# Causal masking by GpSimd and a fused VectorE maximum in place of TensorE's mask products

## The reference

```
x   = table[ids]                                  # (16, 512, 128)
x   = softmax(x W1 (W2 x^T) / sqrt(512)) x        # low-rank mixing, rank 10
two routed experts per sequence (one spatial, one temporal, of 4 each), by the mean token
S   = MHA(LN(x)),        8 heads of 16, no mask   # spatial expert's weights
T   = xt + MHA(LN'(x)),  8 heads of 16, causal    # temporal expert's weights
C   = MHA(q from S, k and v from T), no mask      # shared weights
x   = x + C ;  out = x + MLP(LN(x)), 128 -> 512 -> 128
```

## Time and profile before

| | |
|---|---|
| median of 3 runs | 1761.52 us (1761.07 to 1762.53) |
| profiled execution | 1758.67 us, its span 1756.8 us |
| TensorE busy | 1585.8 us, 90% of the span, 9686 matmuls |
| VectorE busy | 1239.0 us, 71%, 2943 instructions |
| ScalarE busy | 1118.9 us, 64%, 2185 |
| GpSimd busy | 948.1 us, 54%, 1249 |
| mean granted TensorE clock | 0.942 of full speed |

### The profile page before, as it was taken

One profiled execution on the slowest core, in us unless ns is written; L12 is line 12 of the kernel. 1 busy time (PEld: TensorE's weight loads), 2 busy tenths in 40 slices (PEclk: granted clock), 3 DMA queues, 4 the chain that ended last, 5 costly groups with the idle time before them and its releaser, 6 DMA issues. The chain is left out here.

```text
span 1756.8 us, 38227 instructions
## 1 busy us (share of the span) xinstructions
PE 1585.8 (90%) x9686; PEld 728.2 (41%) x9686; DVE 1239.0 (71%) x2943; ACT 1118.9 (64%) x2185; POOL 948.1 (54%) x1249
## 2 busy tenths in 40 slices
PE   3758957999999999999999999999999999975998
PEld 1117942334434444444434444434434444221675
DVE  6886858478687777878687777878687787452442
ACT  3324751747777778777777778687777778724333
POOL 7832443556656656656656656656656655332443
PEclk9768966989999999999999999999999999967999
DMA  2221126356446546546546546546545535030221
GB/s 51 72 48 32 48 57 76 55 71 86 64 67 77 74 54 79 71 55 83 68 63 75 75 55 76 73 56 80 69 65 72 77 50 68 2 37 26 61 65 54
DMA packets 134642, 109.26 MB, mean 62 GB/s; under 512 B 24128, under 2 KB 127552, under 8 KB 134592
## 3 DMA queue, kind: packets, MB, share of 16 engines
q1 hardware_dynamic: 132544, 104.45, 41.0%
q0 software_dynamic: 2048, 4.20, 0.9%
HBM read 19.26 MB, written 8.39 MB: 16 GB/s over the span
## 5 line engine op out<-in xcount | busy, mean ns | idle before, releaser
L1064 ACT ACTIVATE probs<-psum 128x512 f32<-128x512 f32 (+3 forms) x1536 | 744.0, 552 | 315.1 <-PE psum L1178 203.0
L961 DVE TENSOR_REDUCE mx_S<-psum 128x1 f32<-128x512 f32 x512 | 325.0, 682 | 71.4 <-PE psum L1154 69.8
L961 DVE TENSOR_REDUCE mx_C<-psum 128x1 f32<-128x512 f32 x512 | 321.5, 677 | 63.5 <-PE psum L1154 63.5
L961 DVE TENSOR_REDUCE mx_T<-psum 128x1 f32<-128x128 f32 (+3 forms) x512 | 243.1, 488 | 133.2 <-PE psum L1157 122.6
L864 POOL CAST parts_q<-f_q 128x512 bf16<-128x512 f32 x48 | 29.3, 611 | 340.1 <-ACT f_q L1055 340.1
L1154 PE MATMUL psum<-ks_C,qs_C 96*128 96x512 bf16 x512 | 202.2, 398 | 4.9 <-DVE mx_C L961 2.6
L1154 PE MATMUL psum<-ks_S,qs_S 96*128 96x512 bf16 x512 | 199.1, 394 | 5.1 <-DVE mx_S L961 4.1
L1178 PE MATMUL psum<-qs_C,ks_C 99*128 99x512 bf16 x512 | 193.6, 389 | 10.4 <-ACT probs L1064 8.1
L1178 PE MATMUL psum<-qs_S,ks_S 99*128 99x512 bf16 x512 | 194.8, 382 | 2.8 <-ACT probs L1064 0.7
L1178 PE MATMUL psum<-qs_T,ks_T 99*128 99x256 bf16 (+3 forms) x512 | 153.4, 302 | 10.1 <-ACT probs L1064 9.2
L1154 PE MATMUL psum<-ks_T,qs_T 96*128 96x128 bf16 (+3 forms) x512 | 157.0, 308 | 1.1 <-DVE mx_T L961 0.4
(11 more groups left out here) (188 smaller groups left out, 2836.5 us busy)
## 6 DMA issues: line engine op xcount, KB each, us to landing
qs_S<-parts_q SPq DMA_DIRECT2D x96, 128.0 KB, 4.2
ks_S<-parts_k SPq DMA_DIRECT2D x96, 128.0 KB, 4.9
qs_T<-parts_q SPq DMA_DIRECT2D x96, 128.0 KB, 4.4
ks_T<-parts_k SPq DMA_DIRECT2D x96, 128.0 KB, 4.9
qs_C<-parts_q SPq DMA_DIRECT2D x96, 128.0 KB, 4.3
ks_C<-parts_k SPq DMA_DIRECT2D x96, 128.0 KB, 5.0
w_in_S<-in_s_in SPq DMA_DIRECT2D x16, 257.0 KB, 2.7
w_in_T<-in_t_in SPq DMA_DIRECT2D x16, 257.0 KB, 2.6
```

Of the source, the lines that this page charges most:

```text
L961: nc.vector.tensor_reduce(mx[kind][:, n:n + 1], psum[:, ring_place(kind, b, n, RL), 0:last_key], AX_X, ALU.max, negate=True).then_inc(redu ...
L1064: nc.scalar.activation(probs[:, n // 4 % 2, n % 4, t0:T], psum[:, LOGITS + ring_place(kind, b, n, RC), t0:T], ACT.Exp, scale=SCALE).then_i ...
```

## The change

- T's two mask products are gone, and with them the bf16 identity and both triangles.
- For the maxima, VectorE's `reduce` of T is replaced by a fused add and maximum: it adds a tile `causal` (zeros, and in its last 128 columns a triangle of -1e30) to the scores, writes the sums back to the bank, and gives the largest. The sign is turned when the transposed maxima are copied (`keep_maxima`).
- For the probabilities, GpSimd sets the future part of each diagonal block to zero after the exponential (`zero_future`), a whole group of four tiles at once, into a new semaphore `cut` for which T's weighing waits. The eight calls per unit stand between the steps of GpSimd's other work, and `split` is cut into two halves for that.
- The weighing of a group stands nine steps behind its first tile's logits (`WEIGH_AFTER`) where it stood seven; the ring of `probs` has three groups; ScalarE's copies of the sums move from steps 28 and 12 to 30 and 14.
- The sums are copied as ln(scale * x + bias) at once, so that merging adds logarithms (ln 1 = 0 in the rows of the other group), and `reciprocal` is left with one activation.

```diff
 KEPT_AT = (4, 10)
-WEIGH_AT = 3
+WEIGH_AFTER = 9
 VALUES_AT = 16
-GROUP_1_AT, GROUP_2_AT = 28, 12
+GROUP_1_AT, GROUP_2_AT = 30, 14
 SWAP_AT, RECIP_AT = 21, 23
...
 HALF = TILES // 2
-RL, RC = 3, 3
+RL, RC, RP = 3, 3, 3
 
...
     return (TILES * u + n) % ring
+
+
+def group_place(kind, b, q):
+
+    return ring_place(kind, b, 4 * q, 4 * RP) // 4
 
...
         KINDS = "STC"
-        ident_bf = sb("ident_bf", [P, P], BF16)
-        mask_row = sb("mask_row", [P, P], BF16)
-        mask_col = sb("mask_col", [P, P], BF16)
+        causal = sb("causal", [P, T])
         w_in = {k: sb(f"w_in_{k}", [P, IN_COLS]) for k in KINDS}
         w_out = {k: sb(f"w_out_{k}", [P, OUT_COLS]) for k in "TC"}
-        s_outs = sb("s_outs", [P, K, OUT_COLS])
         folds = sb("folds", [P, K, OUT_COLS])
...
         ng_p = sb("ng2_p", [HALF, 2, NPART, P], BF16)
-        probs = sb("probs2", [P, 2, 4, T])
+        probs = sb("probs2", [P, RP, 4, T])
+        s_outs = probs[:, RP - 1, 0:K, 0:OUT_COLS]
         u_all = sb("u_all", [P, T])
...
         s_right = sb("s_right", [P, T])
-        s_log = sb("s_log", [P, T])
         s_recip = sb("s_recip", [P, T])
...
 
-                def split(kind, b, *which):
-
-                    if not exists(b):
+                def zero_future(kind, b, q):
+
+                    if kind != "T" or not exists(b):
                         return
-                    for c in which:
+                    pool.wait_ge(exped, TILES * unit_no("T", b) + 4 * q + 4)
+                    pool.sem_inc(cut_seen, 1)
+                    t0 = first_key("T", 4 * q)
+                    diagonal = probs[:, group_place("T", b, q), :, t0:t0 + P]
+                    nc.gpsimd.affine_select(out=diagonal, in_=diagonal, compare_op=ALU.is_ge, fill=0.0, base=0,
+                                            pattern=[[0, 4], [1, P]], channel_multiplier=-1).then_inc(cut, 1)
+
+                def split_high(kind, b, c):
+
+                    if exists(b):
                         n = 2 * unit_no(kind, b) + c
...
                             .then_inc(rem_done, 1)
+
+                def split_low(kind, b, c):
+
+                    if exists(b):
+                        n = 2 * unit_no(kind, b) + c
                         pool.wait_ge(rem_done, n + 1)
...
                     (kn, bn), (ka, ba), (kb, bb), (ko, bo) = units(i, slot)
-                    split(kn, bn, 0)
+                    zero_future(ko, bo, 5)
+                    zero_future(ko, bo, 6)
+                    split_high(kn, bn, 0)
+                    zero_future(ko, bo, 7)
+                    split_low(kn, bn, 0)
                     split_maxima(kb, bb, 1)
-                    split(kn, bn, 1)
+                    split_high(kn, bn, 1)
+                    zero_future(kb, bb, 0)
+                    split_low(kn, bn, 1)
+                    zero_future(kb, bb, 1)
                     if exists(bo):
...
                         nc.gpsimd.tensor_tensor(u_all[:], u_all[:], u_high[:], ALU.add).then_inc(u_merged, 1)
+                    zero_future(kb, bb, 2)
                     split_maxima(ka, ba, 0)
+                    zero_future(kb, bb, 3)
                     if slot == 0 and exists(i - 1):
...
                             .then_inc(o_ready, 1)
+                    zero_future(kb, bb, 4)
                     if slot == 1 and exists(i + 1):
...
                 affine(xn, 0, 0, "xn")
-                nc.gpsimd.memset(mask_row[:], 0.0)
-                nc.gpsimd.memset(mask_col[:], 0.0)
+                nc.gpsimd.memset(causal[:], 0.0)
                 for k in KINDS:
...
                 last.then_inc(ones_in, 1)
-                split("S", 0, 0, 1)
+                for c in range(2):
+                    split_high("S", 0, c)
+                    split_low("S", 0, c)
                 pool.wait_ge(ones_in, 1)
-                nc.gpsimd.affine_select(out=mask_row[:], in_=mask_row[:], compare_op=ALU.is_ge, fill=NEG, base=0,
-                                        pattern=[[-1, P]], channel_multiplier=1).then_inc(consts, 1)
-                nc.gpsimd.affine_select(out=mask_col[:], in_=mask_col[:], compare_op=ALU.is_ge, fill=NEG, base=0,
-                                        pattern=[[1, P]], channel_multiplier=-1).then_inc(consts, 1)
+                nc.gpsimd.affine_select(out=causal[:, T - P:T], in_=causal[:, T - P:T], compare_op=ALU.is_ge, fill=NEG,
+                                        base=0, pattern=[[-1, P]], channel_multiplier=1).then_inc(masks_made, 1)
                 affine(xt, 0, 1, "xt")
...
                 nc.vector.memset(ks["S"][RA:P, :, :], 1.0)
-                nc.vector.tensor_copy(ident_bf[:], ident[:])
 
...
                     dve.wait_ge(scored, TILES * u + n + 1)
-                    last_key = P * (n % NB + 1) if kind == "T" else T
-                    nc.vector.tensor_reduce(mx[kind][:, n:n + 1], psum[:, ring_place(kind, b, n, RL), 0:last_key], AX_X, ALU.max,
-                                            negate=True).then_inc(reduced, 1)
+                    tile = psum[:, ring_place(kind, b, n, RL), :]
+                    if kind == "T":
+                        dve.sem_inc(scored_seen, 1)
+                        last_key = P * (n % NB + 1)
+                        nc.vector.tensor_tensor_reduce(tile[:, 0:last_key], tile[:, 0:last_key],
+                                                       causal[:, T - last_key:T], 1.0, NEG, ALU.add, ALU.max,
+                                                       mx[kind][:, n:n + 1]).then_inc(reduced, 1)
+                    else:
+                        nc.vector.tensor_reduce(mx[kind][:, n:n + 1], tile, AX_X, ALU.max, negate=True).then_inc(reduced, 1)
 
...
                     at_least(dve, neg_step[half], NEG_STEPS * u)
-                    nc.vector.tensor_copy(ng[:, half, :], desk[0:HALF, 0:P]).then_inc(desk_free, 1)
+                    nc.vector.tensor_scalar(ng[:, half, :], desk[0:HALF, 0:P], -1.0 if kind == "T" else 1.0, None, ALU.mult)\
+                        .then_inc(desk_free, 1)
 
...
                     dve.wait_ge(s_merged, u + 1)
-                    at_least(dve, logged, u)
+                    at_least(dve, recip, u)
                     settle(nc, scrap)
...
                     if n % 4 == 0:
-                        at_least(act, summed, 8 * u + n // 4 - 1)
-                    nc.scalar.activation(probs[:, n // 4 % 2, n % 4, t0:T], psum[:, LOGITS + ring_place(kind, b, n, RC), t0:T], ACT.Exp,
+                        at_least(act, summed, 8 * u + n // 4 - RP + 1)
+                    nc.scalar.activation(probs[:, group_place(kind, b, n // 4), n % 4, t0:T], psum[:, LOGITS + ring_place(kind, b, n, RC), t0:T], ACT.Exp,
                                          scale=SCALE).then_inc(exped, 1)
...
                     at_least(act, u_merged, u)
-                    nc.scalar.activation(s_high[:], sums, ACT.Copy, scale=low[:])
+                    nc.scalar.activation(s_high[:], sums, ACT.Ln, bias=high[:], scale=low[:])
                     nc.scalar.activation(u_high[:], sums, ACT.Copy, scale=high[:]).then_inc(high_out, 1)
...
                     act.wait_ge(swapped, u + 1)
-                    nc.scalar.activation(s_log[:], s_right[:], ACT.Ln).then_inc(logged, 1)
-                    act.wait_ge(logged, u + 1)
                     at_least(act, o_ready, u)
-                    nc.scalar.activation(s_recip[:], s_log[:], ACT.Exp, scale=-1.0).then_inc(recip, 1)
+                    nc.scalar.activation(s_recip[:], s_right[:], ACT.Exp, scale=-1.0).then_inc(recip, 1)
 
...
                             at_least(act, swapped, u)
-                            nc.scalar.activation(s_all[:], sums, ACT.Copy, scale=high[:])
+                            nc.scalar.activation(s_all[:], sums, ACT.Ln, bias=low[:], scale=high[:])
                             at_least(act, o_ready, u)
...
                     keys = P * (tb + 1) if kind == "T" else T
-                    last = nc.tensor.matmul(psum[:, ring_place(kind, b, n, RL), 0:keys], qs[kind][0:RA, hd, P * tb:P * tb + P],
-                                            ks[kind][0:RA, hd, 0:keys], start=True, stop=True)
-                    if kind == "T":
-                        last = nc.tensor.matmul(psum[:, ring_place(kind, b, n, RL), P * tb:keys], ident_bf[:], mask_row[:],
-                                                start=False, stop=True, skip_group_check=True)
-                    last.then_inc(scored, 1)
+                    nc.tensor.matmul(psum[:, ring_place(kind, b, n, RL), 0:keys], qs[kind][0:RA, hd, P * tb:P * tb + P],
+                                     ks[kind][0:RA, hd, 0:keys], start=True, stop=True).then_inc(scored, 1)
 
...
                     bank = LOGITS + ring_place(kind, b, n, RC)
-                    last = nc.tensor.matmul(psum[:, bank, t0:T], ks[kind][0:RB, hd, P * s:P * s + P],
-                                            qs[kind][0:RB, hd, t0:T], start=True, stop=True)
-                    if kind == "T":
```

(23 more changed lines are left out.)

8 lines of the change are left out of this document (5 added, 3 removed).

## The result

| | before | after |
|---|---|---|
| median of the runs, us | 1761.3 (1760.9 to 1762.5, 4 runs) | 1741.27 (1739.2 to 1742.7, 4 runs) |
| ratio, 95% interval | | 0.9884 [0.9867, 0.9901] |
| profiled execution, its span, us | 1758.67, 1756.8 | 1742.72, 1740.9 |
| one turn of the loop, us | 78.92 | 77.71 |
| slots that score S, T, C, us | 26.04, 26.43, 26.46 | 27.27, 25.48, 24.97 |

The kernel is 20 us faster where I forecast 61. Slots are measured from TensorE's first score of a unit to its first score of the next, as a mean over the turns between 430 and 1400 us; the three of a turn are its length.

The account below looks back on a forecast made before the run. TensorE was taken to set the pace. Mask products 3.65 plus recovered idle 0.70 less fused-maximum charge 0.50 gave 3.85 us per batch, times 16 is 61.6; 1758.67 less that, plus 2.85, gave 1700 us, range 1672 to 1745.

Parts of the forecast that it names:

- the factor of 16: Whole kernel: the gain of 3.85 us per batch was multiplied by 16 batches, giving 61.6 us.
- The gain fits, with nothing to spare; the weighing products move two tiles later.: C slot, tiles 16 to 31: without 0.91 us of masks 11.09 is left, just what VectorE needs; weighing columns stay 1280.
- Rest: under 1 us.: Prologue: one cast and two small selects dropped, one memset added; under 1 us, not counted.
- Mask products, 3.65 us a batch.: TensorE: 64 mask products at 0.057 us go; 1.82 us in T slot, 1.37 in C, 0.46 in S.
- Recovered idle, 0.7 with ends 0 and 1.76: TensorE: of 1.76 us idle per batch, 0.7 comes back through fewer logarithms and the shifted weighing.
- own range of 1682 to 1716: Kernel time if the forecast holds: recovered idle 0 to 1.76, T-slot charge 0 to 1; chance 0.66.
- Fused maximum, charge 0.5: T slot: VectorE's fused maximum not quite covered around tiles 16 to 21; 0.5 us lost per batch, ends 0 and 1.82.
- tile cost: VectorE, T slot: fused add-and-maximum plus readout cost 0.61 to 0.73 us per tile, taken as 0.64.
- Rivals B and C: B: VectorE sets the T slot, 1729 us, chance 0.10. C: fused form at half rate, about 1848 us, chance 0.10.
- GpSimd: Eight diagonal-block selects per batch at 0.65 us each; outputs reach TensorE 0.5 to 1.5 us early, thin cover.
- Rival A: GpSimd late in feeding TensorE because selects take near 1.2 us: 1722 us, with follow-ups to 1735; chance 0.12.
- What would show it: Right: T slot 25 us, batch 75. Wrong: fused rows over 0.8 us, TensorE waiting on GpSimd, or idle above 3.

Follow-up runs that it names:

- place of the code: Changed kernel with 100 semaphore increments (fillers) on VectorE, run once ahead of the loop: 1722.23 us, ratio 0.9777.
- copy behind the transpose: Changed kernel with VectorE's copy of the second half of the maxima at step 6 instead of 5: 1729.46 us, ratio 0.9824.
- start: Changed kernel with VectorE's wait for the mask tile moved behind its prologue work, directly ahead of the loop: 1736.23 us, ratio 0.9856.
- the mended kernel: Changed kernel with fillers ahead of the loop, later maxima copy and later mask-tile wait together: 1709.87 us (100 fillers), 1702.74 us (40 fillers).
- 40 fillers: Changed kernel with all three mends, using 40 one-time VectorE semaphore increments ahead of the loop in place of 100: 1702.74 us, ratio 0.9691.
- fillers of 0 and of 128: Changed kernel as it stood, and with 128 one-time VectorE semaphore increments ahead of the loop: 1741.27 us and 1734.79 us.
- the run without fetches: Kernel before with only T's fused maximum replacing the score masks, plus 60 one-time VectorE semaphore increments ahead of the loop: 1736.02 us, ratio 0.9884.

## Why the prediction was wrong

The direction and the range held; the time was 41 us off. Each mend alone, by its ratio times 1761.3 and against the 1740.9 of the change, gives 18.8 (place of the code), 10.6 (copy behind the transpose) and 4.9 us (start, of which the trace shows 3.0); together 34 to 36 us. The other 5 to 7 lie in the factor of 16: the turn of the mended kernel is 3.77 us shorter, which would be 60.3, but from the first score to the last unit's it takes 1160.9 us (40 fillers) where the kernel before took 1215.5, which is 54.6. The first and last turns, which stand outside the loop, gain less than a steady one.

- *Steps that I did not have.* The working counted what each instruction costs and never how many there are in the loop. The order listing showed two entries per fused tile, I used them for the duration of the readout, and the readout cost nothing while its place in the code cost 1.7 us a turn: S slot 27.27 against 25.57. The Trainium skill, "Advanced Engine Details and Errata", section "ISA Cache", says that engines other than TensorE hold two lines of 256 instructions. It would have been a rival, since 312 is above one line and 248 below. The trace agrees that there is a limit, not with those units: by two lines of 256, fillers of 0 and of 128 could not both miss with a body of 312, and they did (88 and 90 packets).
- *"The gain fits, with nothing to spare; the weighing products move two tiles later."* I followed the moved weighing on TensorE by its columns. I did not ask who waits for the instruction it was moved past. That was VectorE's copy of the maxima, 0.8 us in every slot, 1.0 us a turn.
- *"Rest: under 1 us."* The small GpSimd work of the start was counted as busy time and not as a wait ahead of VectorE: 3.0 us.
- *Mask products, 3.65 us a batch.* The condition "if TensorE stays the pace everywhere" doesn't hold: 2.18 in place. The T slot gave 1.54 of 1.82, C and S 0.65 of 1.83. A distance between starts prices a product where TensorE is pressed, not where it is about to wait.
- *Recovered idle, 0.7 with ends 0 and 1.76.* Under-sized, and its upper end was wrong in kind. The logarithms gave 0.90 and the later weighing 1.61, 2.51 together, more than all idle of the earlier trace rows, since a wait also hides where rows overlap less than they could. This error and the last one nearly cancel: 3.65 + 0.70 - 0.50 came out at 3.85 and the mended kernel at 3.77. It was a right sum by two wrong terms, which is luck. The own range of 1682 to 1716 was also narrower than its named ends, which add up to some 1675 and 1719.
- *The parts don't add.* Later weighing, logarithms and fused maximum alone make 1.61 + 0.90 + 1.30 = 3.81, all that the mended kernel has, with nothing left for the logits masks. Which of the four is worth less in company is not shown. No masks at all with the later weighing, and without the logarithm sums, ends at 75.10 too. What holds a turn near 75.1 was not tested: TensorE itself has only 1.61 us idle of 75.20 in the windows of the mended kernel, so it may still be the pace.
- *Fused maximum, charge 0.5.* By chance right: the masks of T's scores are 32 x 0.057 = 1.82, less 0.5 is 1.32, and the run without fetches gave 1.30. But leaving all masks out gave the T slot 1.54, so in place the fused form costs about 0.25. The tile cost was over-sized, 0.64 against 0.44 from start to start: I gave an overlap away that stayed, and charged a readout that runs beside the next tile. Rivals B and C had nothing behind them.
- *GpSimd.* Right: 637 ns a select, 1.7 us of TensorE's waits on it in the whole run, T and C slots in time. Rival A did not occur.
- *What would show it.* I had named TensorE's idle above 3 us per batch as a sign. It is 1.84 + 0.52 + 1.09 = 3.45 in the windows after, and the largest is in the slot of which I had said least.

## What to carry to other kernels

Before costing an edit inside a loop, count the instructions per turn on each engine, semaphore steps and readouts included, and look at the instruction queue's packets over one steady turn: any there at all, and a stall at the jump named after an innocent semaphore, mean that the code is fetched again. The sequencer's branch row on the loop's line and the row behind it show how long it stands; a few fillers ahead of the loop, or a shorter body, tell at once. When a step is moved, list what it is moved past on its queue and who reads that, on every engine. Price a removed product in the kernel by leaving it out, and don't take idle time as the most that a schedule change can give back.
